# Weighted sum of a token attention: the products' layout in SBUF turned, so that VectorE reads its addends side by side

## What is computed

```python
kx = modulated_linear(x, s, k_aff_w, k_aff_b, k_w, k_b)
kx = kx.reshape(B, N, H, D)                    # H = 16 heads, D = 16 features
q = k = v = kx
scores = jnp.einsum('bnhd,bnjd->bnhj', q, k) / math.sqrt(D)
A = jax.nn.softmax(scores, axis=-1)
out = jnp.einsum('bnhj,bnjd->bnhd', A, v).reshape(B, N, F)   # this sum
out = modulated_linear(out, s, o_aff_w, o_aff_b, o_w, o_b)
```

## Time and profile before

| | |
|---|---|
| median of three runs | 3171.58 us |
| profiled execution | 3169.16 us, of which the span 3167.4 |
| TensorE busy | 2413.1 us (76%) |
| VectorE busy | 1562.1 us (49%) |
| ScalarE busy | 1037.9 us (33%) |
| GpSimd busy | 830.2 us (26%) |
| mean granted TensorE clock | 0.789 of full |

### The profile page before, as it was taken

One profiled execution on the slowest core, in us unless ns is written; L12 is line 12 of the kernel. 1 busy time (PEld: TensorE's weight loads), 2 busy tenths in 40 slices (PEclk: granted clock), 3 DMA queues, 4 the chain that ended last, 5 costly groups with the idle time before them and its releaser, 6 DMA issues. The chain is left out here.

```text
span 3167.4 us, 33541 instructions
## 1 busy us (share of the span) xinstructions
PE 2413.1 (76%) x11754; PEld 1587.2 (50%) x11754; DVE 1562.1 (49%) x3728; ACT 1037.9 (33%) x2567; POOL 830.2 (26%) x583
## 2 busy tenths in 40 slices
PE   6258877777777767877777777855999597979798
PEld 5134444444444444544444444533777357574747
DVE  2468567466565765745755754422000144444443
ACT  2024343343343334334234334321222151515050
POOL 0435243153153134225224321020000223232220
PEclk9567886877777677688688688677999797979787
DMA  3000100110020010010020010022222302020200
GB/s 144 35 15 1 55 21 1 42 43 1 10 75 1 9 58 18 9 56 21 1 64 21 1 55 21 1 69 82 90 90 90 103 1 65 3 59 9 56 12 14
DMA packets 66386, 120.48 MB, mean 38 GB/s; under 512 B 29621, under 2 KB 43947, under 8 KB 63795
## 3 DMA queue, kind: packets, MB, share of 16 engines
q1 hardware_dynamic: 53434, 76.51, 7.2%
q0 software_dynamic: 12800, 41.95, 4.8%
HBM read 97.36 MB, written 21.07 MB: 37 GB/s over the span
## 5 line engine op out<-in xcount | busy, mean ns | idle before, releaser
L1022 ACT ACTIVATE att_buf<-att_buf,nmin 128x384 f32<-128x384 f32 (+3 forms) x512 | 288.3, 563 | 854.2 <-DVE nmin L1344 854.0
L858 PE MATMUL bank<-kk,qT 32*128 32x512 f32 (+2 forms) x1024 | 352.7, 725 | 92.1 <-DVE nmin L1344 92.0
L690 POOL TENSOR_TENSOR big<-ex_at,kx 128x2048 f32<-128x2048 f32 x64 | 236.6, 3705 | 428.1 <-DVE xt_na L1131 354.3
L885 PE MATMUL bank<-ident,att_buf 128*128 128x128 f32 x1280 | 254.0, 339 | 22.3 <-ACT att_buf L1030 19.2
L639 POOL TENSOR_TENSOR big<-kx 128x1280 f32<-128x1280 f32 x64 | 162.7, 2570 | 311.1 <-ACT kx L957 303.2
L1131 DVE TENSOR_REDUCE xt_na<-big 128x64 f32<-128x1024 f32 x128 | 240.8, 1899 | 2.2 <-POOL big L690 1.6
L1333 DVE TENSOR_TENSOR att_buf<-bank,wdiag 128x128 f32<-128x128 f32 x384 | 93.0, 284 | 288.9 <-PE bank L863 286.2
L899 PE MATMUL bank<-att_buf,vp 128*32 128x128 f32 x2560 | 234.0, 323 | 0.0
L1030 ACT COPY att_buf<-bank 128x384 f32<-128x384 f32 (+3 forms) x512 | 208.8, 410 | 21.8 <-PE bank L899 17.3
L885 PEld LDWEIGHTS bank<-ident,att_buf 128*128 128x128 f32 x1280 | 187.2, 179 | 33.8 <-ACT att_buf L1022 23.1
L858 PEld LDWEIGHTS bank<-kk,qT 32*128 32x128 f32 x1024 | 117.4, 234 | 165.7 <-DVE nmin L1344 124.5
(11 more groups left out here) (333 smaller groups left out, 4525.1 us busy)
## 6 DMA issues: line engine op xcount, KB each, us to landing
ew<-in_eW SPq DMA_DIRECT2D x16, 1024.0 KB, 8.4
buf_d<-gac SPq DMA_DIRECT2D x16, 320.0 KB, 2.8
eb<-buf_d SPq DMA_DIRECT2D x8, 640.0 KB, 3.6
y_d<-yy SPq DMA_DIRECT2D x8, 640.0 KB, 10.7
xt_na<-in_xT SPq DMA_DIRECT2D x8, 512.0 KB, 3.6
nA<-in_xN SPq DMA_DIRECT2D x8, 512.0 KB, 4.4
x_d<-x SPq DMA_DIRECT2D x8, 512.0 KB, 4.2
kf<-x_d SPq DMA_DIRECT2D x8, 512.0 KB, 3.2
```

The lines of the kernel that those rows point to most:

```text
L690: pool.tensor_tensor(pv[:, :, c * P:(c + 1) * P].rearrange("p o (h d) -> p o h d", d=DH), spread(ex[:, t, :, 8 * c:8 * c + 8], 3, DH), spr ...
L858: pe.matmul(bank[u % 2][:, 0:n], qT[r:r + 32, g, i * P:(i + 1) * P], kk[r:r + 32, g, T * i * P:T * i * P + n], start=True, stop=False)
L885: mm = pe.transpose(bank[3 + u % 2][:, j * P:(j + 1) * P], pr[:, u % NPR, j * P:(j + 1) * P], ident[:])
L1022: act.activation(pr[:, u % NPR, 0:n], pr[:, u % NPR, 0:n], ACT.Exp, scale=-1.0, bias=nmin[:, u % 4:u % 4 + 1], accum_out=rsum[:, i, h:h + ...
```

## The change

The buffer is laid out with the shift innermost: element (f, o) at word 16 f + o. GpSimd walks the same elements in the same order as before, o, h, d, and reads its two inputs as before; its output now steps 16 words with each element. VectorE reads 1024 adjacent words in each reduction, 16 addends side by side. Counts, semaphores, slots and sums are the same.

```diff
-                pv = big[:, 0:H * D].rearrange("p (o f) -> p o f", f=D)
+                pv = big[:, 0:H * D].rearrange("p (f o) -> p f o", o=H)
...
-                                            pool.tensor_tensor(pv[:, :, c * P:(c + 1) * P].rearrange("p o (h d) -> p o h d", d=DH),
+                                            pool.tensor_tensor(pv[:, c * P:(c + 1) * P, :].rearrange("p (h d) o -> p o h d", d=DH),
                                                                spread(ex[:, t, :, 8 * c:8 * c + 8], 3, DH), spread(kv, 1, H, DH), ALU.mult)\
                                                 .then_inc(s("pv_ok"), 1)
...
-                                            dve.tensor_reduce(nA1[:, t, c * w:(c + 1) * w], pv[:, :, c * w:(c + 1) * w].rearrange("p o f -> p f o"),
+                                            dve.tensor_reduce(nA1[:, t, c * w:(c + 1) * w], pv[:, c * w:(c + 1) * w, :],
                                                               X, ALU.add).then_inc(s("pv_used"), 1)
```

## The result

The changed kernel has a median of 3114.75 us in four runs (3108.86 to 3121.39), against 3171.11 for the kernel before (3164.23 to 3173.0): a ratio of 0.9827, 95% interval 0.9802 to 0.9852. A later comparison, four more runs of it beside 18 of the kernel before, gave 0.9841 (0.9793 to 0.9889). The forecast was 3133.8, with a range from 3118 to 3190: right in sign, too small in size, and just outside the range. Of its mechanisms the product, the reduction, the first iteration and the count in the six bear out; the second iteration does not. The profiled execution took 3108.86 us, its span 3107.1.

What follows compares the result with a forecast made beforehand. VectorE was taken to set the pace in part of the six router iterations, TensorE elsewhere there. Savings 36.7 + 3.2 + 1.7 = 41.6 us, less 3.8 for products, gave 37.8 and 3133.8 us; range 3118 to 3190.

Steps and rivals of the forecast that it cites:

- The reduction at 1.22 us: VectorE's L1131 reads adjacent addends like L1110 and falls from 1899 to 1216 ns, 0.68 us saved each, 128 times.
- The product at +0.1 us: GpSimd's L690, now writing 16 words apart, takes 0.1 us more; range 0 to 1.8 us.
- 38 products: Products whose lengthening counts: 8 in the first iteration, 30 in the six; at +0.1 us each they cost 3.8 us.
- dearer small step: Skill page's rule against the forecast: if it held for GpSimd's writes, product some 5.2 us, change loses about 15 us.
- The first iteration, 1.7 us: GpSimd alone sets the pace: three gaps go (0.5 us), two last reductions get shorter (1.2 us).
- Each of the six, 6.12 us: Iterations with router work: 9 of 16 reductions count at 0.68 us each, 36.7 us in six.
- The 13th to 16th reductions: Last four reductions in each of the six fall into VectorE's waits for TensorE: nothing saved.
- the stalls: In the six, small VectorE operations stand still until the GpSimd product ends; a reduction releases it, so they move with it.
- the 7th: Reduction under a product in each of the six; L1236 behind it waits for that product's end anyway: nothing saved.
- The second iteration, 3.2 us: TensorE's four waits for VectorE's minima, 3.2 us in all, can go; after that TensorE is the bound.
- Rival C: TensorE's clock stays at the upper level with shorter gaps in the six: 3120 at 2 us an iteration; chance 0.06.
- The sum: Three stages save 36.7 + 3.2 + 1.7 = 41.6 us, less 3.8 for the products: 37.8 us net.

Runs made afterwards that it cites:

- the pair with four transposes: Four extra TensorE transposes ahead of each of 13 score groups of the second iteration, added to the kernel before (3172.78 us) and to the changed one (3108.97 us, one run).
- the kernel before's second trace: The kernel before run once more with no edit: 3167.09 us (10 runs); second iteration's stretch 63.5 us.
- the second, 3127.57: The changed kernel run once more with no edit, for a second trace: 3127.57 us (3111.71 to 3133.11, 4 runs).
- a GpSimd product of 7.66 us: The changed kernel with GpSimd walking head, feature, shift, so output is written side by side and both inputs step: 3290.51 us, ratio 1.0375.

## Why the forecast was right or wrong

**The reduction at 1.22 us:** right (1213 ns).

**The product at +0.1 us:** the step of the write is not paid on top of the reads, as forecast; the size was +0.02. At 38 products the sum gave away 3.0 us too much. The Trainium skill, Vector Engine (DVE) Microarchitecture Reference, section 5.2, measures its dearer small step on VectorE; in GpSimd's writes it is not seen: 16 words apart, they cost 22 ns in 3.7 us.

**The first iteration, 1.7 us:** from first product to division 33.6 us before, 31.6 after: 2.0. Right.

**Each of the six, 6.12 us:** right in sum, but in part by luck, since two errors cancel. The mean body is 139.4 us in the two traces before and 133.8 in the two after: 5.6 each, 34 in all, where the forecast had 36.7 less 3.0. The 13th to 16th reductions are worth nothing, the stalls move with the reduction ahead of them, and the 7th is swallowed. But the 6.05 us up to L789's start are those of the first of the six. Over all six that part went from 85.8 to 78.8 us on average, 7.0, while the granted clock in it rose from 0.62 to 0.70. Behind L789's start, where the forecast let TensorE's own work run as before, it went from 53.6 to 55.0 us, 1.4 longer.

**The second iteration, 3.2 us:** wrong, and this is the step that failed. The sum let VectorE's shorter reductions count only for TensorE's four waits for minima, took those as gone, and kept TensorE's own work as the bound. None of the three holds. The waits did not go: 3.2 us before and 3.2 after. VectorE's time counted beyond them: about 4 us at an equal granted clock, 6.5 us in the pair with four transposes. And TensorE's own work, 58.98 us in the trace, was no floor: 27 us of it ran at the lower level, behind a wait of 1.19 us that the change removes, and it came out at 46.05. The stretch got 8.6 us shorter against the kernel before's second trace, 11.2 against its first. The forecast's reading that VectorE has hardly a gap there was wrong too: in that stretch it waited 12.2 us for TensorE's score matmuls.

Rival C named the clock, but put it into the six iterations and gave it 0.06. The clock did rise there: in the six bodies TensorE's busy time fell from 629 to 604 us in sum, and the granted clock went from 0.71 to 0.76. No run separates its part; with the 1.4 us behind L789 the six came out at what the count of reductions gave. (C's value at 2 us an iteration should be 3122, not 3120.)

**The sum:** with 2.0, 8.6 and 34 the three stages give 44.6 us. Between the two profiled executions there were 60.3: 2.0 + 11.2 + 36.2 (bodies) make 49.4, 8.6 are the ninth iteration's, and 2.3 are spread over the rest. The medians of the first comparison are 56 us apart, the second comparison's ratio makes 50. The range's lower end, 3118, missed the first median by 3 us; the second, 3127.57, lies inside it. So of the 19 us between forecast and first median the three stages explain about 7 (44.6 against 37.8), mostly the second iteration; the rest lies in code that the edit does not touch. The forecast also took 0.2% as what a measurement can tell; single runs of the kernel before ranged from 3156.6 to 3189.2 us in the later comparisons.

**Left open:** the lead of the six iterations, 661 to 680 us in sum, was shorter on average with the new layout (661.1 to 674.6, mean 667, in seven traces with it in all or three of four tiles of the six; 669.0 to 679.8, mean 674, in seven without). Nothing in it is changed, the ranges overlap, and no run tells whether that is chance.

## What to carry to other kernels

Where two engines wait for one another in turn, the waits of the one do not say what a shorter instruction on the other is worth: here the waits stayed at 3.2 us and the stretch got 8.6 us shorter. Ask also what clock the waiting engine's own work ran at in the trace: its busy time is no floor where it ran at the lower level. A step belongs on the side where it costs nothing: here the same turn of the layout cost GpSimd 0.02 us as an output step and 3.9 us as an input step, and saved VectorE 0.69 us twice for each product. An engine whose product blocks another engine's small operations has a price many times its own time, so count the blocked operations before trading with it.

## What the runs showed of the hardware

A VectorE operation on 32 elements stood still for a GpSimd product of 7.66 us until it ended (4.29 us in place of 0.30, ending within 0.1 us of the product); the reductions ran beside such products at their usual length (mean 1214 ns in that kernel). Code that nobody touched takes different times from run to run: the ninth iteration took 199.6 to 210.4 us, layer 1 640 to 661 us. In the two traces of the changed kernel the granted clock went with it: 0.81 and 0.77 in the ninth iteration (200.5 and 210.4 us), 0.83 and 0.81 in layer 1. In the ninth of the kernel before it was 0.80 at 209 us, so the clock is not all of it.
